# GpSimd's part of an attention step behind both of VectorE's roundings, with the low half of the normalised rows ahead of the un-roundings

## What is computed

```python
def _L0_xattn_ref(x, weight):
    xq = quant_dequant_act_1x128(x)
    wq = quant_dequant_weight_128x128(weight)
    return jnp.einsum('emk,enk->emn', xq, wq)

x = x + _L0_xattn_ref(_layernorm(x, axis=-1), ctx_2048)
x = x + _L0_ffn_ref(_layernorm(x, axis=-1), gate_w, w_gate, w_up, w_down, sw_gate, sw_up, sw_down)
```

## Time and profile before

| | us |
|---|---|
| median of three runs | 6591.76 |
| the profiled execution | 6590.12 |
| its span, first to last instruction | 6588.2 |
| TensorE busy | 6347.2 |
| GpSimd busy | 2900.1 |
| VectorE busy | 2004.7 |
| ScalarE busy | 1330.1 |

### The profile page before, as it was taken

One profiled execution on the slowest core, in us unless ns is written; L12 is line 12 of the kernel. 1 busy time (PEld: TensorE's weight loads), 2 busy tenths in 40 slices (PEclk: granted clock), 3 DMA queues, 4 the chain that ended last, 5 costly groups with the idle time before them and its releaser, 6 DMA issues.

```text
span 6588.2 us, 89812 instructions
## 1 busy us (share of the span) xinstructions
PE 6347.2 (96%) x32166; PEld 3137.9 (48%) x32167; DVE 2004.7 (30%) x2640; ACT 1330.1 (20%) x1976; POOL 2900.1 (44%) x2388
## 2 busy tenths in 40 slices
PE   2999999999999999999999999999999999999998
PEld 1555544445554444444444444444444444444443
DVE  7888533211112222232222222232222332223220
ACT  2666622110001111111111111111111111111111
POOL 4444523732002444454445444454444545445453
PEclk9999999999999999999999999999999999999999
DMA  2455544544335555666666565676655666667653
GB/s 87 154 156 155 178 129 88 122 108 132 109 98 152 158 159 159 164 177 176 168 171 166 164 159 158 166 196 178 170 161 158 184 192 170 168 164 187 180 151 94
DMA packets 1122342, 1015.67 MB, mean 154 GB/s; under 512 B 875504, under 2 KB 877808, under 8 KB 1122288
## 3 DMA queue, kind: packets, MB, share of 16 engines
q1 hardware_dynamic: 177920, 437.40, 20.3%
q10 hardware_dynamic: 838720, 241.77, 19.5%
q0 software_dynamic: 105648, 335.82, 16.5%
HBM read 623.21 MB, written 210.14 MB: 126 GB/s over the span
## 4 chain that ended last, share of the span: by engine, by line
PE 73%; POOL 6%; issue 5%; DVE 5%; DMA 4%; ACTq 3%; ACT 3%; POOLq 0%; DVEq 0%; SPq 0%
PE ps_gu L766 48%; PE ps_d L766 23%; DMA out<-s_out,y_now 3%; PE ps_d L969 2%; ACTq L1228 2%; POOL s_out L701 1%; POOL list_rows L652 1%; POOL hid L711 1%; ACTq L1246 1%; POOL hid_hl L716 1%; ACT wts L1117 1%; DVE wts L1452 1%; DMA xT<-xin 1%; POOL s_out L694 1%; ACT dout L1262 1%
## 5 line engine op out<-in xcount | busy, mean ns | idle before, releaser
L766 PE MATMUL ps_gu<-wts,xT 128*128 128x512 f16 (+1 forms) x20304 | 3950.6, 356 | 24.4 <-DMA xT<-xin 8.2
L766 PEld LDWEIGHTS ps_gu<-wts,xT 128*128 128x128 f16 x20304 | 1993.4, 98 | 1947.1 <-issue 27.4
L766 PE MATMUL ps_d<-wts,hT 128*128 128x512 f16 x7968 | 1768.1, 380 | 23.4 <-ACT dout L1262 11.9
L1594 DVE TENSOR_SCALAR wts<-stage 128x1408 f16<-128x1408 f32 (+2 forms) x447 | 427.6, 957 | 3180.8 <-PE ps_d L969 2995.4
L766 PEld LDWEIGHTS ps_d<-wts,hT 128*128 128x128 f16 x7968 | 778.8, 98 | 956.8 <-issue 38.7
L701 POOL TENSOR_TENSOR s_out<-s_out,dout 128x1024 f32<-128x1024 f32 x208 | 529.7, 2547 | 1218.9 <-ACT dout L1262 1215.8
L1596 DVE SCALAR_TENSOR_TENSOR wts<-stage,wts 128x1408 f16<-128x1408 f32 (+2 forms) x447 | 735.7, 1646 | 15.4
L1232 ACT ACTIVATE sil<-ps_gu 128x704 f32<-128x704 f32 (+2 forms) x272 | 199.1, 732 | 2023.8 <-PE ps_gu L766 2023.6
L1262 ACT ACTIVATE dout<-ps_d,lists 128x1024 f32<-128x1024 f32 x208 | 231.8, 1114 | 1349.7 <-issue 1338.3
L1238 ACT ACTIVATE hid_hl<-hid 128x704 f16<-128x704 f32 (+2 forms) x272 | 207.9, 764 | 1284.8 <-POOL hid L711 1224.0
L711 POOL TENSOR_TENSOR hid<-hid,sil 128x704 f32<-128x704 f32 x208 | 348.5, 1675 | 131.7 <-ACT hid L1266 127.4
(11 more groups left out here) (167 smaller groups left out, 2650.4 us busy)
## 6 DMA issues: line engine op xcount, KB each, us to landing
stage<-in_L_ffn_w_down SPq DMA_DIRECT2D x384, 256.0 KB, 4.4
stage<-in_L_ffn_w_gate SPq DMA_DIRECT2D x256, 352.0 KB, 4.0
stage<-in_L_ffn_w_up SPq DMA_DIRECT2D x256, 352.0 KB, 5.6
wts<-in_x SPq DMA_DIRECT2D x64, 512.0 KB, 3.7
rows_x<-wts SPq DMA_DIRECT2D x64, 512.0 KB, 3.2
xT<-cols_x ACTq DMA_DIRECT2D x63, 512.0 KB
wts<-in_ctx SPq DMA_DIRECT2D x32, 512.0 KB, 4.0
cols_x<-xT SPq DMA_DIRECT2D x32, 512.0 KB, 4.7
```

Of the source, the lines that this page charges most:

```text
L766: ins = nc.tensor.matmul(dst[c], left, right[c], start=(first and a == 0), stop=(last and a == 2))
L1594: v.tensor_scalar(high, raw, WSCALE, 1.0, ALU.mult, ALU.mult).then_inc(cast_done, 1)
```

## The change

Three things change in GpSimd's program. `beside(i)` begins with a wait for `rounded[CTX]`, the later of VectorE's two roundings of the step before. `low_of_x2` moves from the end of `beside(i)` to its start, and so from tile i to tile i-1: it now stands behind `add_slice(i-3)`, in the tail behind the splits, and ahead of L585, L589 and L599. The loop is cut into three loops with the same body. The last two tiles' low halves are placed in steps 30 and 31. No instruction of a data path is added or taken away.

```diff
--- before.py
+++ after.py
@@ -602,13 +602,15 @@
                 pool.wait_ge(x2_high, i + 1)
                 g.tensor_tensor(x2nat[:, 1, :], x2f, x2nat[:, 0, :], ALU.subtract).then_inc(x2_ready, 1)
 
-            def beside(i, ctx=True, x2=True):
-
+            def beside(i, ctx=True, x2=True, low=None):
+
+                if ctx:
+                    pool.wait_ge(rounded[CTX], i + CLEAD)
+                if x2:
+                    low_of_x2(i - 1)
                 dequantise_x(i + (LEAD - 1))
                 if ctx:
                     unround_ctx(i + (CLEAD - 1))
-                if x2:
-                    low_of_x2(i)
 
             for c in range(BT):
                 unround_ctx(c)
@@ -619,9 +621,15 @@
             pool.wait_ge(conv_done, CHUNKS_S)
             pool.sem_inc(s_ready, 1)
             beside(-1, x2=False)
-            beside(0)
+            beside(0, x2=False)
             beside(1)
-            with pool.Fori(2, TT - CLEAD + 1) as i:
+            with pool.Fori(2, BT) as i:
+                beside(i)
+                add_slice(i - 2)
+            with pool.Fori(BT, 2 * BT) as i:
+                beside(i)
+                add_slice(i - 2)
+            with pool.Fori(2 * BT, TT - CLEAD + 1) as i:
                 beside(i)
                 add_slice(i - 2)
 
@@ -629,6 +637,8 @@
                 if i < TT - LEAD + 1:
                     beside(i, ctx=False)
                 else:
+                    low_of_x2(i - 1)
+                if i == TT - 1:
                     low_of_x2(i)
                 if i < TT - 1:
                     add_slice(i - 2)
```

## The result

The changed kernel takes 6610.0 us, the median of 7 runs (6600.0 to 6622.0), against 6590.0 for the kernel before (7 runs, 6581.7 to 6598.8): a ratio of 1.0034, 95% interval 1.0022 to 1.0046. It is 20 us slower, where 30 us faster was forecast; the range ended at 6582. The profiled execution took 6607.13 us, its span is 6605.2.

A forecast was written before the change was run, and what follows sets the result against it. VectorE's order of work was taken to bound the attention stage, TensorE most of the rest. Terms -42.7 + 3.9 + 2.1 + 7 = -29.7 us, from 6590.1 profiled or 6591.8 median, gave 6561 us, range 6546 to 6582.

The forecast's parts named there:

- the 1.94 us: Main attention steps: VectorE's second rounding waits for GpSimd's L603, so two roundings take 4.29 us instead of 2.35.
- -42.7 us: Main attention steps: 22 steps each shortened by 1.94 us on VectorE's loop once L603 moves away.
- +3.9 and +2.1: Given back where VectorE waits for TensorE: 3.9 us at batch starts (steps 8, 16), 2.1 us after step 21.
- R: The end of VectorE's two roundings (L1452) in a step, where the next step's `ctx_max` starts.
- The store of the normalised rows on SP's queue moves ... Nothing.: Main steps: store moves from R - 0.8 to R + 3.6; transfers behind it wanted over 13 us away, cost nothing.
- The tail, +7 us: Steps 24 to 31: GpSimd's longer queue costs about 5 us, ScalarE's wait at tile 29 2; between +3 and +12.
- GpSimd in time in the main steps: GpSimd's L599 ends about R + 10.2, before VectorE needs it at R + 12.96: slack 2.7 us, no cost.
- Rival 4: Main steps: GpSimd's queue runs late through `add_slice` waiting for `s_out`, taking 1.3 us of each step's gain: 6585, chance 0.06.
- Rival 1: Main steps: TensorE becomes the bound as its clock still falls, each step gaining 1.0 us: 6579, chance 0.12.
- Rival 3: Main steps: the hold moves to VectorE's one-column instructions under L599, losing 2.4 us a step: 6607, chance 0.05.
- Rival 2: TensorE's lead is worth nothing and the tail costs little: 6555 or 6551, 0.15 of the forecast's own chance.
- Rival 5: Little changes: main-step gain given back at the batches and in the tail (+12 and half the gain): 6589, chance 0.05.

The follow-up runs named there:

- e4: The kernel before with the change in the main steps alone, plus the context tile's load ahead of the x tile's on SP's queue: 6549.0 us.
- e3: The changed kernel with the context tile's load ahead of the x tile's on SP's queue: 6587.6 us.
- e8: The kernel before with only the context tile's load put ahead of the x tile's on SP's queue: 6590.2 us.
- e7: The changed kernel with the weight loads of steps 24 to 27 ahead of the store of normalised rows on SP's queue: 6592.5 us.
- e9: The changed kernel with the stores of normalised and transposed rows one step later in SP's tail, behind x1 store and residual load: 6587.2 us.
- e10: The kernel before with SP's weight loads of steps 24 to 27, and transfers behind them, held until the next step's un-rounding L585: 6611.9 us.
- e11: e4 with one of the two splits of a tail step moved ahead of the low half on GpSimd: 6550.5 us.

## Why the prediction was wrong

Sign and range were wrong. Point by point:

- **What bounds the kernel, and the 1.94 us.** Right. VectorE's order was the clock, L603 held the second rounding, and both roundings took 2.35 us once it was gone.
- **The sum's first term, -42.7 us, with +3.9 and +2.1 behind it.** Right for a kernel with the loads swapped: 36.7 us were forecast up to there, and e4 has 683.7 - 646.6 = 37.1, with a step of 21.96 us and waits of 2.17 us for TensorE at steps 8 and 16. In after it was half, 18.7 us. The missing step: I asked whether GpSimd is in time for the new, earlier R, but not whether every other input of the work at R is. `ctx_max` reads a tile that a DMA brings. No row of waits showed that load, since it was early, by 1.1 us in the mean; with `ctx_max` 1.94 us earlier it is 0.8 us late, and the trace shows 0.77. e3, e4 and e8 show that it is this load.
- **"The store of the normalised rows on SP's queue moves ... Nothing."** This is the step that turned the sign. It looked at who wants the stored rows and at the two transfers behind, and only in the main steps. In the tail, where the low half went behind 9 us of splits, I asked nothing about SP at all, though the prediction had its queue in view in the main steps. Four weight loads, a store and a load stand behind that store; let go together they meet the transpose. e7, e9 and e10 show it, with 17, 26 and 19 us.
- **The tail, +7 us.** Its mechanism on GpSimd was right, +1.46 us a step against +0.9 to +1.5. But the term had only GpSimd's queue and 2 us for ScalarE's wait at tile 29, and its upper bound was 12; it measured 41.0 us, and 14.8 without the burst. Two waits for the low half are new: ScalarE's `normalise_l` (19.0 us, expected only at tile 29, it comes in six steps) and TensorE's `tr_x2` (10.9 us), of which the text ahead of the prediction says that it comes two steps later, and which has no term. ScalarE's wait for the store of the transposed rows (8.9 us) is new too. How the 14.8 divide between these and the queue wasn't tried apart.
- **GpSimd in time in the main steps.** Right: L599 ends at R + 10.8, and L1432 did not wait for GpSimd between 204 and 660 us. Rival 4 falls.
- **Rival 1, TensorE's clock.** The granted clock in 204 to 660 us was 1.00, against 0.97 before. It falls. TensorE's wait for `ctx_max` was forecast at 15 us there: 28.1 in after, where `ctx_max` itself is late, and 14.4 in e4.
- **Rival 3, the one-column instructions.** L1483 took 0.21 us, as before. It falls for the one-column instructions of the main steps; e11 shows that VectorE's TENSOR_SCALAR of eight columns are held beside GpSimd's splits, 0.17 us becoming up to 2.08. My only price on the slower side, 6607, was near the result for a reason that did not happen. The Trainium skill, "SBUF — State Buffer", section "Who interferes with whom", also says that a VectorE instruction with two SBUF inputs contends with a GpSimd instruction that reads SBUF; the roundings (2.16 us against 1.22) agree.
- **Rival 2, TensorE's lead worth nothing.** It took TensorE's lead to cost nothing: VectorE waited 4.5 us for L776 in the main steps (7.7 in e4), where it said none. It falls.
- **Rival 5, little changes.** It had the right shape, a gain given back in the tail, with tail +12 as its worst case.

The chance of 0.07 for slower was the real fault of the numbers: the tail's bound of +12 was built from terms that I had found, and nothing in it stood for the queue that I had costed at nothing without a row.

## What to carry to other kernels

When a bound of x us a step is taken away, list every input of the instruction that now starts earlier, DMA loads too, and write down how early each was: one that was early by less than x is the next bound, and the waits of the profile do not show it. When an instruction is moved to a later place on its engine, follow whoever waits for it on an in-order DMA queue and then everything behind that wait, in each stage apart: a held queue lets its transfers go in a burst (eight in 4.9 us here), and the burst pays where a short transfer on the critical path comes next. Test the parts of such an edit apart: here one half was worth -20 us, the other +33, and keeping the first with one pair of loads swapped gave -40.

## What the runs showed of the hardware

I had not expected a small transfer to suffer that much from those on another engine's queue. The transpose on ScalarE's queue landed in 2.4 us (median of 700 to 900 us) in before, where SP's transfers were spread, and in 5.8 us in after, where up to eight of them were issued in the 5.5 us ahead of it, though the DMA engines' share over the 200 us was lower (0.49 against 0.57). Its issue instruction got longer too, 1.22 to 1.53 us, and 2.31 in e10. The Trainium skill, "DMA: Bandwidth & Descriptors", section "Queues, rings and completion order", says that each DMA engine takes turns between the queues it has work for, a packet at a time; the late landings fit that, and show what it cost a transpose here.

TensorE's granted clock often fell with its waits here. The eight matmuls on `hT` took 3.19 us behind a wait of 4.55 us in after (granted clock 0.57), 3.60 behind 5.92 in e10 (0.50), and 1.90 behind 1.62 in e7 (1.00): the last at 2.4 GHz throughout, those of e10 at 1.2, those of after mostly at 1.2. The wait alone does not decide it: in one step of before they took 3.23 us behind 2.15 (0.57), in the next 1.90 behind 1.61, and in another step of e7 1.90 behind 2.52 (1.00). Over 700 to 900 us the mean granted clock was 0.92, against 0.96 before. So part of what a late transpose costs is paid in the matmuls behind it.

e11 shows VectorE held beside GpSimd in instructions that are short when alone: 0.90, 0.97 and 2.08 us instead of 0.17, for eight columns each. The reciprocal of eight columns between them took 0.19 us, as in e4, and a one-column TENSOR_SCALAR took 0.21 us also beside L560 (at 745.61 in e11). So the idle time of GpSimd there was not free to fill.
